# Graph attention on one core: a row of four edges in DRAM of 3088 bytes for 3136

## The chip, the cores and the metric

The kernel runs on one core of a Trainium2 chip. The metric is the device time of one execution in microseconds (us). A core has a matrix engine (TensorE, PE), a vector engine (VectorE, DVE), an engine for pointwise functions (ScalarE, ACT), a general one (GpSimd, POOL) and SyncE (SP), which here only issues transfers. 16 DMA engines move data between DRAM and the on-chip memory of 128 partitions.

## The reference

6250 nodes of 96 features, 200,000 edges (src, dst). Each edge takes a query from its source node and a key and a value from its target node; the softmax over the edges of a source node weighs the values.

```python
q = (embeds[rows] @ qW).reshape(e, HEADS, dh)      # rows = src, 4 heads of 24
k = (embeds[cols] @ kW).reshape(e, HEADS, dh)      # cols = dst
v = (embeds[cols] @ vW).reshape(e, HEADS, dh)
scores = jnp.clip(jnp.einsum('ehd,ehd->eh', q, k), -10.0, 10.0)
exp_s = jnp.exp(scores)
norms = jax.ops.segment_sum(exp_s, rows, num_segments=nvar)[rows]
w = exp_s / (norms + 1e-08)
res = jax.ops.segment_sum(w[:, :, None] * v, rows, num_segments=nvar).reshape(nvar, d)
...
x = _layernorm(x + embeds + res)                   # embeds is x
```

The edges come sorted by dst. The sums are over src, so the kernel sorts them again.

## The kernel before

**Part one (to about 170 us).** x is projected to q, k and v. k and v go to a table in DRAM (`kv3`), q stays on chip. At the same time the edges are counted by tile of 128 source nodes. SP also clears the last block of each of 49 tiles in `rows_dram` with 49 transfers of `pad_rows` (`clear`), a tensor of one row a partition.

**Part two (to about 840 us).** 112 groups of 1792 edges, two groups a turn, 56 turns. Every edge gets a place: edges of the same tile lie together, in runs of four (`RUN`). For each group a window of 128 table rows is loaded (`window_of`, L798, 144 KB; SP issues it once PE is done with the window before it), and the local numbers of the targets are broadcast to all partitions (L822, 1024 KB a turn). PE picks k and v by matmuls with a 0/1 matrix (L1188), ACT writes them from PSUM into `payload` (L937) and beside them the tag, the source node's number in its tile (L933). `payload` holds for two turns (p) and two groups (u) 16 columns of `WROW` floats on each partition: k, v (2 x 96 floats), the tag at `TAG` = 192, and what is left up to `WROW`. Four columns, one run, are one row in DRAM: `rows_dram` has `RUN * WROW` floats a row. POOL scatters them with an indirect DMA (L654), 128 rows each, four to a group, eight to a turn, 448 in all. A group's `payload` is written again two turns later, once its scatters have landed.

**Part three (from about 840 us).** The 472 blocks of 128 rows are read in 236 pairs (L842, 392 KB each, ring `blk` of 8 pairs, a place free when POOL's message of its last pair is made). For each pair ACT copies the tags (L972), DVE makes the 0/1 matrix of tags (L1611), PE turns it (L1261) and fetches q (L1271), DVE forms q times k (L1625) and sums it (L1634), ACT takes exp (L979), POOL multiplies v by it (L716), PE sums over the edges (L1250) and DVE adds the sums to `acc` (L1601). Each step runs some pairs behind the one before (`lagged`). At the end the layer norm and the stores.

All of `work`'s tiles, `payload` and `blk` among them, are cut one behind the other out of one tensor, so that those behind them begin where they end. Before its first scatter POOL waits for the table and the clears, sets the floats of `payload` behind the tag to zero (L635) and waits for that.

Of the kernel before, what the change touches and what calls it, by code (L numbers as in the profile page):

```python
# [25 lines left out]
P = 128  # L26
# [5 lines left out]
COLS = 14  # L32
QUAD = 2
RUN = 4
RB = 4
NCH = RB * RUN
HC = 2
KPART = 4
TSLOT = 4
WROW = 196  # L40
TAG = 192
BLK = 4
PAIR = 2
# [18 lines left out]
def gnn_program(nc, x, src, dst, wq, wk, wv, out):  # L62
# [3 lines left out]
    NT = -(-N // P)  # L66
# [12 lines left out]
    KPARTS = NCH // KPART  # L79
# [3 lines left out]
    NBLK = NPAIR * PAIR  # L83
    FULL = MOST_RUNS // P
    NBATCH = NG // HG
    PIECES = NBATCH // PB
# [12 lines left out]
    TI = FULL_NT // TSLOT  # L99
# [6 lines left out]
    assert COLS * P + (RUN - 1) * NB <= RUNS * RUN <= 2048 and SORTED < FAR and NBLK < 2048  # L106
    assert RUN == 1 << RUN_BITS and P == 1 << P_BITS and NCH == KPARTS * KPART and EDGE_ROWS < ITERS - 1
    assert NG == HG * NBATCH and NBATCH % PB == 0 and NB <= HI * LO and HROWS <= P and TT <= P and NT <= CLEARS * (TI + 1)
    assert RB == KPARTS and RUN == KPART and FULL + NT <= NBLK and FULL <= 512 and PIECES == 7 and TI == 12 and COLS * P <= 2048


    HEAD_SLOT = 1
# [8 lines left out]
    kv3 = nc.dram_tensor("kv3_table", (NTAB, 3 * 2 * D), BF16).ap()  # L121
    rows_dram = nc.dram_tensor("sorted_rows", (SORTED, RUN * WROW), F32).ap()
    local_dram = nc.dram_tensor("sorted_local", (2, QUAD * NCH, P), F16).ap()

    with ExitStack() as ctx:
        def sb(name, shape, dt):
            return ctx.enter_context(nc.sbuf_tensor(name, shape, dt))

        def sem(name):
            return ctx.enter_context(nc.semaphore(name))  # L130
# [21 lines left out]
        blk_row = sb("blk_row", [P, NBLK], F16)  # L152
        pad_rows = sb("pad_rows", [P, RUN * WROW], F32)

# [26 lines left out]
        def share(at, shape, dt):  # L181
            n = 1
            for d in shape:
                n *= d
            words = -(-n // 2) if dt in (BF16, F16) else n
            assert at + words <= WORK, (at, words)
            top[0] = max(top[0], at + words)
            v = work[:, at:at + words]
            v = v if dt == F32 else v.bitcast(dt)
            v = v[:, 0:n]  # L190
            if len(shape) == 1:
                return v, at + words
            names = " ".join(f"d{i}" for i in range(len(shape)))
            return v.rearrange(f"p ({names}) -> p {names}",
                               **{f"d{i}": d for i, d in enumerate(shape)}), at + words


        payload, at = share(0, [2, QUAD, NCH, WROW], F32)
        far_rows, at = share(at, [NCH // 2, 2, 3, D], BF16)
# [88 lines left out]

        blk, at = share(0, [SBI, PAIR, BLK, WROW], F32)
        tags, at = share(at, [SBI, CH, TWIN], BF16)  # L290
# [7 lines left out]

        sq_all, _ = share(SBI // 2 * PAIR * BLK * WROW, [NT, D], F32)
        assert NT * D <= SBI // 2 * PAIR * BLK * WROW and NPAIR <= SBI * (JS - 1) + SBI // 2  # L300
        inv = pad_rows[:, 0:NT * HEADS].rearrange("p (t h) -> p t h", t=NT)
# [56 lines left out]
        pads_made = sem("pads_made")  # L358
# [198 lines left out]
        def _(pool):  # L557
# [74 lines left out]
                pool.wait_ge(table_out[n], 16 * (TI // 2))  # L632
            pool.wait_ge(rest_out, 32)
            pool.wait_ge(tails_out, 16 * NT)
            pool.memset(payload[:, :, :, :, TAG + 1:WROW].rearrange("p o u c w -> p (o u c) w"), 0.0).then_inc(pads_made, 1)  # L635
            pool.wait_ge(pads_made, 2)
            last_place = pool.to_reg(SORTED - 1)
            last_row = pool.to_reg(NTAB - 1)

# [1092 lines left out]
```

## Time and profile before

| | |
|---|---|
| median of 3 runs | 1666.95 us (1665.98 to 1668.39) |
| profiled execution | 1672.0 us, its span 1670.2 us |
| PE busy | 1465.2 us, 88% |
| DVE busy | 1431.4 us, 86% |
| ACT busy | 1019.1 us, 61% |
| POOL busy | 912.8 us, 55% |
| moved by the DMA engines | 465.03 MB, mean 278 GB/s |

Busy shares are means over parts with different limits, so the parts have to be read one by one. The granted clock of PE was 0.95 of full speed in the mean.

### The profile page before, as it was taken

The numbers are of one execution on the slowest core, as the hardware profiler recorded it, in microseconds if no ns is written. First come the engines' busy times: TensorE is split into PE (matmuls) and PEld (weight loads), VectorE is DVE, ScalarE is ACT, GpSimd is POOL, SyncE is SP. The second block draws the span as 40 slices with busy tenths as digits, with TensorE's granted clock in tenths as the row PEclk, the third lists the DMA queues.
The fourth block names the chain that finished last, engine by engine and source line by source line (L and its number), as shares of the span: only waits on it lengthen the run. The fifth ranks groups of instructions, "written<-read, shape, count | busy, mean of one in ns | idle before, by whom it ended". The sixth has DMA issues, their size and how long they took to land.

```text
span 1670.2 us, 56304 instructions
## 1 busy us (share of the span) xinstructions
PE 1465.2 (88%) x19964; PEld 1407.4 (84%) x19965; DVE 1431.4 (86%) x2940; ACT 1019.1 (61%) x1836; POOL 912.8 (55%) x768
## 2 busy tenths in 40 slices
PE   5854988898888888888769999999999999999992
PEld 3744878787787878888769999999999999999992
DVE  5889999898988998899258888888888888888897
ACT  4342666566666665666546666666666666666665
POOL 6240777677767777777734444444444444444442
PEclk8566999999999999999979999999999999999996
DMA  7672999999999999899979767677777777777742
GB/s 222 221 274 102 352 367 354 346 331 374 355 328 357 358 357 338 348 364 355 351 286 299 240 241 246 237 248 240 243 247 238 244 245 239 246 242 240 247 157 58
DMA packets 159483, 465.03 MB, mean 278 GB/s; under 512 B 37026, under 2 KB 59298, under 8 KB 152276
## 3 DMA queue, kind: packets, MB, share of 16 engines
q1 hardware_dynamic: 120916, 300.70, 54.2%
q0 software_dynamic: 35840, 163.36, 24.1%
q10 hardware_dynamic: 2688, 0.46, 0.2%
q8 instruction: 23, 0.38, 0.1%
q14 instruction: 16, 0.13, 0.0%
HBM read 271.21 MB, written 209.73 MB: 288 GB/s over the span
## 4 chain that ended last, share of the span: by engine, by line
PE 76%; DVE 10%; issue 7%; DMA 4%; SPq 1%; ACT 1%; DVEq 0%; POOL 0%; POOLq 0%; ACTq 0%
PE two_a L1188 13%; PE meta L1250 13%; PE sum_bank L1250 12%; PE two_b L1188 11%; PE two_a L1271 7%; PE two_b L1271 7%; PE one_d L1261 3%; PE one_c L1261 3%; DMA work<-kv_table 2%; PE meta L1206 2%; PE one_d L1217 2%; DVE work L1523 1%; DVE work L1530 1%; PE sum_bank L1170 1%; DVE cols_work L1368 1%
## 5 line engine op out<-in xcount | busy, mean ns | idle before, releaser
L654 POOL DMA_INDIRECT sorted_rows<-work x448 | 498.9, 1114 | 210.4 <-issue 144.5
L716 POOL TENSOR_TENSOR work<-work 128x768 f32<-128x768 f32 x236 | 352.2, 1492 | 440.7 <-ACT work L979 440.7
L1188 PE MATMUL two_a<-work 128*128 128x192 bf16 x2688 | 265.1, 249 | 88.6 <-issue 86.1
L1188 PEld LDWEIGHTS two_a<-work 128*128 128x128 f16 x2688 | 217.0, 99 | 109.5 <-issue 89.5
L937 ACT ACTIVATE work<-two_a 128x768 f32<-128x768 f32 x224 | 181.5, 810 | 150.0 <-PE two_a L1188 148.2
L1188 PE MATMUL two_b<-work 128*128 128x192 bf16 x2688 | 264.7, 250 | 0.0
L988 ACT ACTIVATE work<-work 128x1024 f32<-128x1024 bf16 x236 | 247.2, 1048 | 0.0
L1250 PE MATMUL sum_bank<-work 128*128 128x100 f32 x1888 | 235.9, 278 | 3.6 <-DVE acc L1601 3.6
L1250 PE MATMUL meta<-work 128*128 128x100 f32 x1888 | 235.9, 278 | 0.9 <-DVE acc L1601 0.9
L1634 DVE TENSOR_REDUCE work<-work 128x32 f32<-128x768 f32 x236 | 225.0, 953 | 8.2
L1188 PEld LDWEIGHTS two_b<-work 128*128 128x128 f16 x2688 | 223.1, 99 | 6.3
L1250 PEld LDWEIGHTS sum_bank<-work 128*128 128x128 f32 x1888 | 219.8, 192 | 4.0 <-issue 3.9
L1250 PEld LDWEIGHTS meta<-work 128*128 128x128 f32 x1888 | 219.6, 192 | 1.3 <-issue 1.2
L979 ACT ACTIVATE work<-work 128x32 f32<-128x32 f32 x236 | 54.1, 229 | 261.6 <-DVE work L1618 261.6
L937 ACT ACTIVATE work<-two_b 128x768 f32<-128x768 f32 x224 | 181.7, 811 | 46.4 <-PE two_b L1188 45.3
L1611 DVE TENSOR_TENSOR work<-work,node_row 128x1024 bf16<-128x1024 bf16 x236 | 163.4, 692 | 20.6 <-ACT work L972 20.6
L1625 DVE TENSOR_TENSOR work<-two_a,work 128x768 f32<-128x768 f32 x118 | 113.0, 958 | 41.7 <-PE two_a L1271 41.6
L1625 DVE TENSOR_TENSOR work<-two_b,work 128x768 f32<-128x768 f32 x118 | 113.0, 958 | 40.8 <-PE two_b L1271 40.8
L1271 PE MATMUL two_a<-q,work 128*128 x2832 | 141.1, 207 | 2.3 <-ACT work L985 2.3
L1271 PE MATMUL two_b<-q,work 128*128 x2832 | 140.3, 207 | 0.0
L1271 PEld LDWEIGHTS two_a<-q,work 128*128 128x128 bf16 x2832 | 129.5, 98 | 3.1 <-issue 2.9
L1271 PEld LDWEIGHTS two_b<-q,work 128*128 128x128 bf16 x2832 | 129.2, 98 | 0.0
(235 smaller groups left out, 2186.6 us busy)
## 6 DMA issues: line engine op xcount, KB each, us to landing
work<-sorted_rows SPq DMA_DIRECT2D x472, 392.0 KB, 3.5
work<-sorted_local SPq DMA_DIRECT2D x56, 1024.0 KB
sorted_rows<-pad_rows SPq DMA_DIRECT2D x49, 392.0 KB, 4.6
work<-kv_table SPq DMA_DIRECT2D x112, 144.0 KB
sorted_rows<-work POOLq DMA_INDIRECT x448
kv_table<-work SPq DMA_DIRECT2D x12, 576.0 KB, 3.4
work<-in_x SPq DMA_DIRECT2D x12, 192.0 KB, 4.4
out<-acc SPq DMA_DIRECT2D x6, 384.0 KB
```

Source lines behind the costliest of these rows:

```text
L654: pool.indirect_dma_start(out=rows_dram, out_offset=bass.IndirectOffsetOnAxis(ap=place_now[:, p, u, b:b + 1], axis=0), in_=payload[:, p, u ...
L716: pool.tensor_tensor(now[:, :, 0:D].rearrange("p c (h f) -> p c h f", h=HEADS), blk[:, k, :, :, D:2 * D].rearrange("p m c (h f) -> p (m c) ...
L937: act.activation(payload[:, p, u, KPART * part:KPART * (part + 1), 0:2 * D].rearrange("p (b k) w -> p b k w", b=2), kv_ps[part % 2], ACT.C ...
L979: act.activation(msg[:, k % MSGS, :, D:AW], clipped[:, k], ACT.Exp).then_inc(exp_made[k % PSEM], 1)
L988: act.activation(hot_f[:, k % HOTF], hot[:, k % HOTS], ACT.Copy).then_inc(hotf_made[k % PSEM], 1)
L1188: mm = pe.matmul(to, picked[:, u % 2, k * P:(k + 1) * P], window[:, u, :, n, :], start=(n == 0), stop=(n == 2))
L1250: mm = pe.matmul(sums[k % 2][:, m, :], hot_f[:, k % HOTF, m * BLK + c, :], msg[:, k % MSGS, m * BLK + c, :], start=(c == 0), stop=(c == BL ...
L1261: mm = pe.transpose(turned[k % 2][:, c, :], hot[:, k % HOTS, c, :], ident_b[:])
L1271: mm = pe.matmul(q_ps[k % 2][:, m, c, :], hot_T[:, k % 2, m * BLK + c, :], q3[:, bass.ds(tile, 1), i, :].rearrange("p a d -> p (a d)"), st ...
L1611: dve.tensor_tensor(hot[:, k % HOTS].rearrange("p c (n i) -> p c n i", i=TWIN), tags[:, k].unsqueeze(2).to_broadcast([P, CH, P // TWIN, TW ...
L1625: dve.tensor_tensor(qk.rearrange("p (m c) d -> p m c d", m=PAIR), q_ps[k % 2], blk[:, k, :, :, 0:D], ALU.mult).then_inc(qk_made[k % PSEM], 1)
L1634: dve.tensor_reduce(score[:, k], qk.rearrange("p c (h f) -> p (c h) f", h=HEADS), AX.X, ALU.add).then_inc(score_made[k % PSEM], 1)
```

## The change

An edge's row is 193 floats, k, v and tag, for 196. Four of them are 772 floats (3088 bytes) for 784 (3136 bytes). With that `payload`, `blk`, `pad_rows` and `rows_dram` shrink, and everything cut out behind them moves. The memset of the floats behind the tag, and POOL's wait for it, are gone. An assertion keeps `WROW` at `TAG + 1`.

```diff
@@ -37,7 +37,7 @@
-WROW = 196
+WROW = 193
 TAG = 192
...
-            pool.memset(payload[:, :, :, :, TAG + 1:WROW].rearrange("p o u c w -> p (o u c) w"), 0.0).then_inc(pads_made, 1)
-            pool.wait_ge(pads_made, 2)
             last_place = pool.to_reg(SORTED - 1)
             last_row = pool.to_reg(NTAB - 1)
```

No instruction changes its place. POOL's program ahead of its first scatter, before; 784 is the length of a row in floats:

```order
L630 TENSOR_LOAD flag_i [waits tables_made]
L630 ISA x2
L635 MEMSET work 128x64x3 [waits rest_out,tails_out,table_out1,table_out0]
L700 COMPARE_AND_BRANCH [waits pads_made]
L701 UNCONDITIONAL_BRANCH
L701 ISA
L654 DMA sorted_rows<-work 60416x784 [waits place_made0,tag_kept0,pay0_made0]
L654 DMA sorted_rows<-work 60416x784 [waits pay1_made0]
```

And in the changed kernel, where lines from 635 on stand two lines higher:

```order
L630 TENSOR_LOAD flag_i [waits tables_made]
L630 ISA x2
L698 COMPARE_AND_BRANCH [waits rest_out,tails_out,table_out1,table_out0]
L699 UNCONDITIONAL_BRANCH
L699 ISA
L652 DMA sorted_rows<-work 60416x772 [waits place_made0,tag_kept0,pay0_made0]
L652 DMA sorted_rows<-work 60416x772 [waits pay1_made0]
```

The memset and the wait for `pads_made` are gone, the waits for the table and the clears stand at the branch, and the scatters carry rows of 772 floats.

## Rows read from the trace of the kernel before

**Rows 1.** The page: tenths of DMA share in 40 slices of the span, and GB/s.

```profile
DMA  7672999999999999899979767677777777777742
GB/s 222 221 274 102 352 367 354 346 331 374 355 328 357 358 357 338 348 364 355 351 286 299 240 241 246 237 248 240 243 247 238 244 245 239 246 242 240 247 157 58
```

**Rows 2.** Stretches of the span: busy us and instructions of each engine, granted clock, DMA.

```profile
core 0: us, PE busy (x) PEld busy (x) DVE busy (x) ACT busy (x) POOL busy (x), PEclk, DMA share, GB/s
0.00:130.00 130.00, 84.59 (x308) 65.01 (x309) 100.84 (x148) 56.74 (x71) 55.41 (x77) 0.68 0.70 240
...
960.00:1600.00 640.00, 640.00 (x9279) 640.00 (x9278) 567.32 (x1160) 425.70 (x774) 288.10 (x194) 1.00 0.71 243
...
200.00:800.00 600.00, 519.26 (x7338) 488.49 (x7337) 539.32 (x1183) 370.79 (x640) 443.04 (x396) 0.98 0.96 352
955.00:1600.00 645.00, 645.00 (x9361) 645.00 (x9360) 571.61 (x1171) 428.49 (x781) 289.74 (x195) 1.00 0.71 243
```

**Rows 3.** The chain that ended last, 955 to 1600 us, shares by line.

```profile
by line: PE sum_bank L1250 27.8%; PE meta L1250 27.8%; PE two_b L1271 15.5%; PE two_a L1271 15.3%; PE one_c L1261 6.8%; PE one_d L1261 6.7%
```

**Rows 4.** Waits from 200 to 800 us: us in total, times, longest.

```profile
ACT work L937 <- PE two_a L1188: 131.7, 183, 4.0
POOL sorted_rows L654 <- issue: 97.0, 294, 2.1
...
PE two_a L1188 <- issue: 75.4, 45, 3.0
ACT work L937 <- PE two_b L1188: 39.5, 191, 1.1
POOL sorted_rows L654 <- DVE work L1502: 35.1, 32, 3.0
...
POOL sorted_rows L654 <- ACT work L937: 25.2, 70, 1.5
```

**Rows 5.** Timeline of one turn: start us, us, instruction, idle before.

```profile
601.00 0.33 SPq L822 DMA_DIRECT2D work<-sorted_local  x1
...
606.73 6.49 SPq L798 DMA_DIRECT2D work<-kv_table  x2
...
614.36 1.15 PE L1188 MATMUL two_a<-work 128*128 128x192 bf16 x12 [1.56 <-issue]
```

**Rows 6.** The page's queue of the scatters: packets, MB, share of 16 engines.

```profile
q0 software_dynamic: 35840, 163.36, 24.1%
```

**Rows 7.** The queue of SP's loads from 955 to 1600 us.

```profile
q1 hardware_dynamic: 56118, 156.47, 71.1%
```

**Rows 8.** The queue of the 8 KB stores from 200 to 800 us.

```profile
q10 hardware_dynamic: 2352, 0.40, 0.4%
```

**Rows 9.** Timeline of POOL around its first scatter.

```profile
130.66 0.26 POOL L635 MEMSET work<- 128x192 f32 x1 [2.53 <-DMA kv_table<-work]
164.64 1.33 POOL L654 DMA_INDIRECT sorted_rows<-work  x1 [33.72 <-issue]
```

**Rows 10.** What SP's queue waited for, 0 to 200 us.

```profile
SPq L777 <- POOL work L620: 64.6, 11, 13.5
```

**Rows 11.** Pieces of the chain at the start of part three: start us, us.

```profile
844.72 6.17 DMA work<-sorted_rows
...
892.94 4.39 DMA work<-sorted_rows
```

**Rows 12.** Groups that read or write edge rows: busy us, mean ns, idle before.

```profile
L716 POOL TENSOR_TENSOR work<-work 128x768 f32<-128x768 f32 x236 | 352.2, 1492 | 440.7 <-ACT work L979 440.7
...
L937 ACT ACTIVATE work<-two_a 128x768 f32<-128x768 f32 x224 | 181.5, 810 | 150.0 <-PE two_a L1188 148.2
...
L1625 DVE TENSOR_TENSOR work<-two_a,work 128x768 f32<-128x768 f32 x118 | 113.0, 958 | 41.7 <-PE two_a L1271 41.6
...
L972 ACT ACTIVATE work<-work 128x16 bf16<-128x16 f32 x236 | 48.8, 207 | 16.1 <-DMA work<-sorted_rows 16.1
...
L933 ACT ACTIVATE work<-work 128x16 f32 (+1 forms) x112 | 25.4, 227 | 35.5 <-DMA work<-sorted_local 31.0 <-ACT work L952 4.5
```

**Rows 13.** Waits from 955 to 1600 us.

```profile
POOL work L716 <- ACT work L979: 355.4, 195, 1.9
```

More of the change, by code:

```diff
@@ L108, in gnn_program @@
     assert NG == HG * NBATCH and NBATCH % PB == 0 and NB <= HI * LO and HROWS <= P and TT <= P and NT <= CLEARS * (TI + 1)
-    assert RB == KPARTS and RUN == KPART and FULL + NT <= NBLK and FULL <= 512 and PIECES == 7 and TI == 12 and COLS * P <= 2048
+    assert WROW == TAG + 1 and RB == KPARTS and RUN == KPART and FULL + NT <= NBLK and FULL <= 512 and PIECES == 7 and TI == 12 and COLS * P <= 2048
     HEAD_SLOT = 1
```

## The prediction

> **What bounds the kernel now.** I read the line of DMA shares over the span first, then the stretches, the chain of waits and the queue tables of two stretches. The run has three parts. Up to 170 us the edges are counted and ordered. From 170 to 840 us the edge rows are built and scattered to DRAM (56 turns, 12 us each). From 840 us on the rows are read back and summed [rows 1, 2].
>
> In the third part PE is busy in all of its 640 us, every step of the chain is a PE group, and the DMA engines work at 0.71 [rows 2, 3]. Whatever a load of rows gains or loses there does not reach the end, as long as the DMA share stays below 1: 147 ns a row (below) could become 207.
>
> In the second part PE is busy 519 of 600 us, DVE 539, POOL 443, and the DMA engines 0.96 of the time at 352 GB/s [rows 2]. The reader should see where PE's missing 81 us stand: 75.4 us lie in 45 waits ahead of L1188, nearly one for each of the 49.5 turns, put down to "issue" [rows 4]. One such wait shows what it is. SP issues the window of the second group at 606.73 us, right after PE ended that group's previous work; PE starts the group at 614.36 us, 1.56 us after it ran dry [rows 5]. A window is 144 KB, and in the same ring stands the broadcast of 1,024 KB issued at 601.00, while POOL puts eight scatters, 163.36 MB / 56 = 2.9 MB, in each turn into the other ring [rows 6]. So PE waits for its window because the 16 DMA engines are full. POOL isn't the limit: its 443.0 us of scatter instructions and 97.0 us of gaps of 0.3 us between them are 540 of 600 us, and it waited 60.3 us for DVE and ACT [rows 2, 4]. Hence a turn is about as long as its DMA work.
>
> **The scatter, the term of the sum.** The scatters' queue (q0) moved 163.36 MB, which is 52,092 rows of 3,136 bytes, and took 24.1% of the engines' span: 0.241 x 1670.2 = 402.5 us [rows 6]. That is 402.5 x 16 / 52,092 = 123.6 ns of one engine a row. A row of 3,088 bytes is 48 bytes, 1.53%, shorter. No row of this trace shows a transfer of rows whose length isn't a multiple of 64 bytes (x rows are 384 bytes, table rows 1,152, broadcast rows 8,192), so I bound it.
>
> - If time goes by bytes in all of it: 402.5 x 0.0153 = 6.2 us less.
> - If a part is a fixed price of a packet: of the 35,840 packets of q0, 448 x 16 are completions, and 28,672 are left, four to an engine and scatter, of 52,092 / 28,672 = 1.82 rows and 402.5 x 16 / 28,672 = 224.6 ns each (two rows, less those out of bounds). The loads of the third part are one row a packet: 0.711 x 645 us x 16 / 49,895 rows (156.47 MB) = 147.1 ns [rows 7]. From row + packet = 147.1 and 1.82 rows + packet = 224.6 come 95 ns for a row and 52 for a packet. This is an estimate, the two stretches having different neighbours. 1.53% of 95 ns is 1.45 ns, and 52,092 x 1.45 / 16 = 4.7 us less.
> - If the engine moves pieces of which the 48 bytes don't save one: 0. Rows of 3,088 bytes start at any multiple of 16 bytes, and touch 49 pieces of 64 bytes wherever they start, as many as 3,136 bytes do.
> - On the other side: each row now begins or ends inside a piece of 32 bytes that it shares with its neighbour. What a write of a part of a piece costs no row shows. The nearest is the smallest packet: queue q10 (256-byte rows and completions) took 0.4% of 600 us on 16 engines for 2,352 packets, 16.3 ns each [rows 8]. One more such piece a row is 52,092 x 16.3 / 16 = 53 us more.
>
> I take 4.7 us, since it is built on the rows nearest to it, both packets of the same row length. Of it the part counts in which the engines are the limit, by their share 0.96: **4.5 us less**, 0.08 us of each turn. PE's wait of 1.6 us a turn is large enough to give it back. When the wait is shorter, PE's own 10.5 us a turn comes next, far off.
>
> **The removed memset, and its wait.** It took 0.26 us, and the first scatter began 33.7 us after it, when the first rows were ready [rows 9]. POOL has nothing else to do in between: 0. It also covers the lost wait for `pads_made`, of which nothing else hangs behind. If this cover were gone it would be 0.26 us and a wait, once.
>
> **The clears.** 49 blocks of pad rows shrink by 0.3 MB in all, in the first part, where the DMA engines work at 0.70 [rows 2] and SP waits for POOL's table parts (64.6 us at L777) rather than for a queue [rows 10]: 0.
>
> **The start of the third part.** Here loads stand on the chain: 6.17 us for the first block and 4.39 us at 893 us, where SP's load of x shares the engines [rows 11]. 1.5% of 10.6 us is 0.2 us less.
>
> **The compute engines.** Rows of an edge now start every 772 bytes for 784, so most no longer start on 16 bytes. Nobody's count of elements changes. L937 writes such rows (810 ns), L716 and L1625 read them (1492 and 958 ns), L933 and L972 touch their tags (227 and 207 ns) [rows 12]. No row shows them off 16 bytes; ends are nothing and, say, their slack. In part two ACT waits 171 us for PE before L937, about 0.43 us for each of its 396, so it may take half as long again. In part three POOL waits 355.4 / 195 = 1.8 us a pair [rows 13], and DVE is idle 73 us of 645, 0.38 us a pair [rows 2]. With PE at 100% none of this is seen: 0. Tiles laid out behind the rows move by 768 bytes, tensors behind `pad_rows` by less; none changes its shape: 0. An odd 0.4 us more in L1625 would be the first thing to show.
>
> **Sum.** 4.5 + 0.2 = 4.7 us less. The profiled execution took 1672.0 us, of which 1670.2 are its span; it would take 1667.3. Taken off the median of the runs, 1666.95 (the profiled one is 0.3% above it), the forecast is 1662.2 us.
>
> **Rivals.**
> A. *The forecast* (time by bytes): 1660.5 to 1663.6. For it speaks the DMA share of 0.96 with PE waiting in nearly every turn; against it, that two thirds of a gain of 0.3% are already enough to vanish below what can be told from no change.
>
> B. *Nothing to measure*, in two ways. The row's time goes by pieces, worth 0 to 3 us. For example, if the engine also handles the bytes between a row's start and the 256-byte boundary below it, the mean start is 96 bytes above it before (rows start at 0, 64, 128, 192) and 120 after (at any multiple of 16), so 3,232 bytes become 3,208; 0.74% of 95 ns is 0.70 ns a row, 2.3 us in all, and the time 1664.6. Or PE's wait is the latency of the window in its ring and not the engines' load; then 1667. Against the latter speaks that a window of 144 KB took 7.6 us [rows 5].
>
> The first of these is a rule of the Trainium skill: "DMA: Bandwidth & Descriptors", section "How a descriptor splits into AXI transactions", has reads fetched from the 256-byte boundary below their start, with unused bytes that still cost. No row of this trace shows whether that is so; the chance of B holds it.
>
> C. *Slower*: the writes of part two now end inside shared pieces, and the memory or the engine must read the piece before it writes. The place is the scatter, 52,092 rows; the third part reads only. It decides from 1.45 + 1.0 = 2.5 ns a row, beyond which the kernel is over 3.3 us slower. At a third of the small packet's price, 5.4 ns, it is 52,092 x 3.95 / 16 = 13 us more, 1680; at the whole price 48 us more, 1715. For it speaks that no write of before met such a piece and that the engines have no idle time in which to hide one [rows 2]; against it, that it is one piece in about 97, and may be read where the engine doesn't wait for it.
>
> The Trainium skill speaks for C in "Collectives: The Full Stack", section "Rules for kernel authors": it asks for buffers aligned to 32 bytes because that prevents a read-modify-write in the hardware. It names no price, and every row written before starts at a multiple of 64, so the trace can't say.
>
> That the change doesn't do what it says can be left out: the scatters and loads have 772 elements a row for 784.
>
> **How the numbers follow.** About 0.2%, 3.3 us, is what a measurement of this kernel can tell from no change. A has 0.42 and is faster. B has 0.30 and lies within. C has 0.28 and is slower, 0.12 of it beyond 1685, since the small packet's price is an upper end. The low end is by bytes in all, 1666.95 - 6.2 - 0.2 = 1660.5, less the 1 us by which runs of one kernel differ: 1659. The high end of 1685 takes in C up to 18 us more (7 ns a row gross), which leaves out 0.12 above and about 0.05 below. The likeliest is A.
>
> **What would show it.** Right: q0's bytes 160.9 MB and its share near 23.8%; the 600 us of part two at the same share 0.96 with 0.08 us less a turn; the first load of rows from DRAM some 5 us earlier than 844.7; all of part three unchanged at 3.31 us a pair, and its DMA share 0.70. Wrong: q0's time a row above 124 ns, with PE's waits before L1188 longer than 75 us in 600 (C); q0's time a row at 123 to 124 ns (B, pieces); q0's share down and the turn unchanged (B, latency); a DMA share well above 0.71 in part three, or PE no longer at 100% there (a cost on the reads that I gave no chance).

## The result: slower, by 0.2 to 0.6%

| | before | changed |
|---|---|---|
| median of 5 runs each | 1668.39 us | 1677.86 us |
| ratio | | 1.0057 (95%: 1.0038 to 1.0075) |
| profiled execution, span | 1672.0, 1670.2 us | 1677.9, 1676.1 us |
| beside each other again, on another chip | 1671.46 us | 1673.85 us |
| ratio | | 1.0021 (1.0007 to 1.0035) |

The forecast was 1662.2 us and faster. Both comparisons have the changed kernel slower; they differ in how much.

The profile of the changed kernel, queue of the scatters on the page (packets, MB, share of 16 engines over the span), the same packets as in [rows 6], 2.5 MB less, and yet more time:

```profile
q0 software_dynamic: 35840, 160.86, 24.4%
```

0.244 x 1676.1 = 409.0 us x 16 / 52,092 rows are 125.6 ns a row, for 123.6 before.

Stretches of the span (columns as in [rows 2]), and the queue of SP's loads from 955 to 1600 us:

```profile
200.00:800.00 600.00, 520.26 (x7301) 489.91 (x7301) 533.80 (x1172) 368.06 (x635) 438.67 (x392) 0.97 0.95 345
955.00:1600.00 645.00, 645.00 (x9362) 645.00 (x9359) 571.38 (x1171) 428.47 (x780) 289.91 (x195) 1.00 0.72 239
```

```profile
q1 hardware_dynamic: 56158, 154.17, 72.4%
```

In these 600 us of part two POOL issued 392 scatters for 396, and the engines moved 345 GB/s for 352 at a share of 0.95 for 0.96. That is this one execution: in another of the same kernel (e6 below) it was 397 scatters and 350 GB/s at 0.96. Part three takes its 3.31 us a pair as before, PE without a gap. But its loads are dearer too: 154.17 MB are 49,926 rows, 0.724 x 645 x 16 / 49,926 = 149.7 ns a row for 147.1 [rows 7]. PE does not wait for that in this stretch.

The groups of the engines have not moved: L714, L935 and L1623 (L716, L937 and L1625 before) take what they took in [rows 12].

```profile
L714 POOL TENSOR_TENSOR work<-work 128x768 f32<-128x768 f32 x236 | 352.7, 1495 | 441.9 <-ACT work L977 441.9
...
L935 ACT ACTIVATE work<-two_a 128x768 f32<-128x768 f32 x224 | 181.6, 811 | 154.4 <-PE two_a L1186 151.2
...
L1623 DVE TENSOR_TENSOR work<-two_a,work 128x768 f32<-128x768 f32 x118 | 112.9, 957 | 41.8 <-PE two_a L1269 41.8
```

Where this execution lost time shows in the scatters' own line (duration ns min/median/max, first and last start in us), first of the kernel before, then of the changed one:

```profile
L654 POOL DMA_INDIRECT sorted_rows<-work x448: 967/975/1907, 164.6 to 839.3; - x150
```

```profile
L652 POOL DMA_INDIRECT sorted_rows<-work x448: 967/975/1905, 164.3 to 843.4; - x150
```

Of 5.9 us by which the span is longer, 4.4 arise between the first and the last scatter, 679.1 us for 674.7. The rest is behind the last scatter. The chain of waits of the changed kernel there (start us, us):

```profile
848.90 6.09 DMA work<-sorted_rows
...
887.24 9.69 SPq L847
...
899.48 4.03 DMA work<-sorted_rows
```

Before, the same issue of x's last rows (L849) stood 7.24 us on the chain, so 2.4 us were lost there in this execution:

```profile
883.15 7.24 SPq L849
```

Two more profiles, e6 (the changed kernel again) and e1 (nearly the same, both below), do not repeat this picture. From the first to the last scatter they took 672.0 and 671.3 us, less than before, and behind the last scatter 835.1 and 835.8 us for 830.9 (the first profile of the changed kernel: 832.7). In both, 3 to 4 us of that is PE busy for longer on the same work, with a granted clock of 0.97 from 900 to 960 us where before it was 1.00. So no place for the loss is shown.

```profile
L652 POOL DMA_INDIRECT sorted_rows<-work x448: 966/976/2706, 164.9 to 836.9; - x150
```

```profile
L652 POOL DMA_INDIRECT sorted_rows<-work x448: 967/976/1930, 164.4 to 835.7; - x150
```

So the question is why 48 bytes less a row, 1.5% of the largest stream of part two, where DMA looked like the limit, save nothing.

### The profile page after: what moved, and what is told of

The parts are those of the page before. It is cut to its first block, busy times and chain, and to the rows that moved or that the text cites. A ratio compares the mean times of both kernels' runs of the same rounds, so it can differ in the third digit from the quotient of the medians.

```text
span 1676.1 us, 56303 instructions
## 1 busy us (share of the span) xinstructions
PE 1465.8 (87%) x19964; PEld 1408.8 (84%) x19965; DVE 1430.6 (85%) x2940; ACT 1018.8 (61%) x1836; POOL 913.3 (54%) x767
## 3 DMA queue, kind: packets, MB, share of 16 engines
q0 software_dynamic: 35840, 160.86, 24.4%
## 4 chain that ended last, share of the span: by engine, by line
PE 79%; DVE 8%; issue 7%; DMA 4%; SPq 1%; ACT 1%; POOL 0%; DVEq 0%; POOLq 0%; ACTq 0%
PE two_a L1186 14%; PE two_b L1186 13%; PE meta L1248 12%; PE sum_bank L1248 12%; PE two_a L1269 7%; PE two_b L1269 7%; PE one_c L1259 3%; PE one_d L1259 3%; DMA work<-kv_table 3%; PE meta L1204 2%; PE one_d L1215 2%; PE sum_bank L1168 1%; DVE cols_work L1366 1%; PE sum_bank L1087 1%; DMA work<-sorted_rows 1%
## 5 line engine op out<-in xcount | busy, mean ns | idle before, releaser
L714 POOL TENSOR_TENSOR work<-work 128x768 f32<-128x768 f32 x236 | 352.7, 1495 | 441.9 <-ACT work L977 441.9
L1186 PEld LDWEIGHTS two_a<-work 128*128 128x128 f16 x2688 | 218.3, 99 | 112.0 <-issue 91.9
L935 ACT ACTIVATE work<-two_a 128x768 f32<-128x768 f32 x224 | 181.6, 811 | 154.4 <-PE two_a L1186 151.2
L935 ACT ACTIVATE work<-two_b 128x768 f32<-128x768 f32 x224 | 181.7, 811 | 47.7 <-PE two_b L1186 46.6
L1623 DVE TENSOR_TENSOR work<-two_a,work 128x768 f32<-128x768 f32 x118 | 112.9, 957 | 41.8 <-PE two_a L1269 41.8
L1623 DVE TENSOR_TENSOR work<-two_b,work 128x768 f32<-128x768 f32 x118 | 113.0, 958 | 40.9 <-PE two_b L1269 40.9
```

The lines of the kernel that those rows point to most:

```text
L714: pool.tensor_tensor(now[:, :, 0:D].rearrange("p c (h f) -> p c h f", h=HEADS), blk[:, k, :, :, D:2 * D].rearrange("p m c (h f) -> p (m c) ...
L935: act.activation(payload[:, p, u, KPART * part:KPART * (part + 1), 0:2 * D].rearrange("p (b k) w -> p b k w", b=2), kv_ps[part % 2], ACT.C ...
L1186: mm = pe.matmul(to, picked[:, u % 2, k * P:(k + 1) * P], window[:, u, :, n, :], start=(n == 0), stop=(n == 2))
L1623: dve.tensor_tensor(qk.rearrange("p (m c) d -> p m c d", m=PAIR), q_ps[k % 2], blk[:, k, :, :, 0:D], ALU.mult).then_inc(qk_made[k % PSEM], 1)
```

## Experiments

Each was run beside the kernel before on one chip; the kernels of one comparison share their runs of before. All of the layouts below except e6, e1, e10 and e14 come out of one rewriting of the changed kernel, in which the four pitches are numbers of their own (below with the changed kernel's values). In e2, e3, e4, e7 and e16 an edge has 193 floats in a run, and what a run or a row has beyond 772 is padding at its end, zeroed once. In e5, e11, e12, e13 and e15 it has 192 and no tag, so that their sums over edges are meaningless, while the instructions keep their sizes. And in e2, e3, e4, e7, e12 and e16 POOL multiplies a pair (L714) in two instructions of half the size, which takes 317 us of the 645 of part three for 290. No run has this split together with the layout of before, so a small difference of these kernels to before can be the split's.

```diff
+PAY_PITCH = 772    # a run of four edges on chip, part two
+BLK_PITCH = 772    # the same, part three
+ROW_PITCH = 772    # a row in DRAM, and what a scatter moves
+LOAD = 772         # what a load of part three moves of it
...
-    rows_dram = nc.dram_tensor("sorted_rows", (SORTED, RUN * WROW), F32).ap()
+    rows_dram = nc.dram_tensor("sorted_rows", (SORTED, ROW_PITCH), F32).ap()
-        payload, at = share(0, [2, QUAD, NCH, WROW], F32)
+        payload, at = share(0, [2, QUAD, RB, PAY_PITCH], F32)
...
-        blk, at = share(0, [SBI, PAIR, BLK, WROW], F32)
+        blk, at = share(0, [SBI, PAIR, BLK_PITCH], F32)
...
-                        in_=payload[:, p, u, b * RUN:(b + 1) * RUN, :].rearrange("p k w -> p (k w)"), in_offset=None,
+                        in_=payload[:, p, u, b, 0:ROW_PITCH], in_offset=None,
```

The expectations weigh theories by letter. D, S: a start off 32 bytes costs, in DRAM or on chip. L: a length that is no multiple of 32 costs. B: the shift of the other tensors costs. G: such a start costs on either side, and a row over 3072 bytes costs one piece more. P: the stretches of 256 bytes touched in DRAM set a row's time. Y: its bytes do. M: only a row of whole such stretches is cheap.

All results together. "Stretches" is the number of 256-byte stretches of DRAM, counted from multiples of 256, that a row touches in the mean over all rows; it is worked out from the pitch, and takes it that the tensor starts on such a multiple, which no trace shows. "Part two" is the time from the start of the first scatter to that of the last, in one profile each. ns are engine time a row from the shares of the two queues in the same profile. The changed kernel and e1 give 124.8 to 125.6 and 149.7 to 150.1, and e5, e10 and e14, whose DMA rows are alike, 120.4 to 122.0 and 146.4 to 147.5: a difference under 1.5 ns says little.

| kernel | bytes a row | stretches | part two, us | scatter, load ns | time to before (95%) |
|---|---|---|---|---|---|
| before | 3136 | 13 | 674.7 | 123.6, 147.1 | 1 |
| changed, again (e6) | 3088 | 13 | 672.0 | 125.3, 149.9 | 1.0021 (1.0007 to 1.0035) |
| e1 | 3088 | 13 | 671.3 | 124.8, 150.1 | 1.0018 (1.0005 to 1.0031) |
| e2 | 3136 | 13 | 675.9 | 123.7, 149.6 | 1.0004 (0.9993 to 1.0015) |
| e3 | 3088 | 13 | 669.8 | 124.1, 148.4 | 1.0014 (1.0002 to 1.0026) |
| e4 | 3104 | 13 | 669.9 | 123.0, 148.3 | 1.0002 (0.9987 to 1.0017) |
| e7 | 3136, loads 3088 | 13 | 673.7 | 123.5, 149.2 | 0.9999 (0.9982 to 1.0016) |
| e16 | 3200 | 13 | 672.9 | 125.7, 152.8 | 1.0044 (1.0026 to 1.0062) |
| e11 | 3008 | 12.5 | 663.9 | 118.8, 146.3 | 0.9955 (0.9941 to 0.9970) |
| e5 | 3072 | 12 | 654.9 | 120.4, 146.4 | 0.9883 (0.9864 to 0.9902) |
| e12 | 3072 | 12 | 652.6 | 120.2, 147.3 | 0.9899 (0.9881 to 0.9917) |
| e15 | 2944 | 12 | 656.3 | 116.3, 142.7 | 0.9883 (0.9861 to 0.9906) |
| e13 | 2816 | 11 | 638.7 | 112.0, 138.1 | 0.9799 (0.9785 to 0.9813) |
| e10 | 3072 | 12 | 654.5 | 122.0, 147.5 | 0.9914 (0.9894 to 0.9933) |
| e14 | 3072 | 12 | 654.0 | 121.4, 147.3 | 0.9894 (0.9876 to 0.9912) |

The scatters' lines of e12, e11, e13 and e16 (those of e5 and e15 stand with their runs):

```profile
L663 POOL DMA_INDIRECT sorted_rows<-work x448: 967/978/1904, 165.3 to 817.9; - x150
```

```profile
L663 POOL DMA_INDIRECT sorted_rows<-work x448: 966/975/1907, 163.9 to 827.8; - x150
```

```profile
L663 POOL DMA_INDIRECT sorted_rows<-work x448: 968/982/1894, 165.1 to 803.8; - x150
```

```profile
L664 POOL DMA_INDIRECT sorted_rows<-work x448: 969/977/1907, 165.5 to 838.4; - x150
```

By stretches, part two took 669.8 to 679.1 us at 13 (nine profiles, the changed kernel's first among them), 663.9 at 12.5, 652.6 to 656.3 at 12 (five profiles) and 638.7 at 11.

### Which side, which length

**e2**, only the starts on chip off 32 bytes:

```diff
+PAY_PITCH = 788
+BLK_PITCH = 788
+ROW_PITCH = 784
+LOAD = 784
```

> Rows in DRAM are 784 floats (3136 bytes, starts at multiples of 64 bytes) and 784 floats are moved, as before; on chip a run of four edges (193 floats each, 12 of padding behind them) starts every 788 floats (3152 bytes), at any multiple of 16 bytes. POOL's message of a pair is two instructions of half the size. Theory D (the start in DRAM costs): a row takes 123.6 ns on the scatters' queue and 147 ns on the loads' in part three, as before, and the time is that of before within 0.2%. Theory S (the start on chip costs): 125.6 and 149.7 ns, 6 to 10 us slower than before. Theory L (the length costs, 3088 bytes being no multiple of 32): as before.

Measured: 1.0004, the scatter at 123.7 ns as before, the load at 149.6 for 147.1. So the load is 2.5 ns dearer, through the starts on chip or POOL's split instruction, and the scatter, which reads there, shows nothing. Theory S falls as the cause of the lost time: the kernel is as fast as before. The queue of loads of e2 from 955 to 1600 us, with the same row length as in [rows 7]:

```profile
q1 hardware_dynamic: 56100, 156.43, 72.3%
```

**e3**, only the starts in DRAM off:

```diff
+PAY_PITCH = 784
+BLK_PITCH = 784
+ROW_PITCH = 772
+LOAD = 772
```

> Rows in DRAM are 772 floats (3088 bytes), as in the changed kernel; on chip a run starts every 784 floats, at a multiple of 32 bytes. Theory D: as the changed kernel, 125.6 ns a row for the scatter, 149.7 for a load, 6 to 10 us slower than before. Theory S: faster than before by 4.5 us, at 122.2 ns a row and 145.7. Theory L: as the changed kernel.

Measured: 1.0014, 124.1 and 148.4 ns. It is not the gain of 4.5 us that S asked for. It is a loss of 2.3 us, less than the 6 to 10 of D. With starts on chip in order, 48 bytes less still save nothing.

**e4**, a row of 3104 bytes, every start in DRAM and of runs on chip on 32 bytes (all pitches 776):

> A row is 776 floats, 3104 bytes or 97 x 32, in DRAM and on chip (193 floats an edge, 4 of padding to a run), so that every start is a multiple of 32 bytes and half of them of 64. Theories D, S and L with a piece of 32 bytes: nothing is shared, and the 32 bytes saved show: 122.6 ns a scattered row, 146 a loaded one, 3 us faster than before. With a piece of 64 bytes: 124.5 to 125.6 and about 149, 4 to 9 us slower.

Measured: 1.0002, 123.0 and 148.3 ns. 32 bytes less and nothing shared in any piece of 32: no loss, and no gain either. Whether the 0.2% that the changed kernel is slower lie between 3104 and 3088 isn't shown, since the intervals overlap.

**e6**, the changed kernel again, and **e1**, the changed kernel with the tensors behind `pad_rows` where they were:

```diff
-        pad_rows = sb("pad_rows", [P, RUN * WROW], F32)
+        pad_rows = sb("pad_rows", [P, RUN * 196], F32)
...
-                    sp.dma_start(of_block(FULL + b), pad_rows[:]).then_inc(tails_out, 16)
+                    sp.dma_start(of_block(FULL + b), pad_rows[:, 0:RUN * WROW]).then_inc(tails_out, 16)
```

> The changed kernel again, beside the others on the chip of this comparison. Theory G (a start off 32 bytes costs on either side, and a row over 3072 bytes costs one piece more): 125.6 ns a scattered row, 149.7 a loaded one, 6 to 10 us slower than before, while the two kernels with only one side off 32 bytes were 0 and 2 us slower. If it is as fast as before here, the first result was the chip's scatter.

> The changed kernel, but with pad_rows as wide as before (784 floats), so that all tensors behind it start where they did, at multiples of 64 bytes rather than 32 bytes past one. Rows are 3088 bytes in DRAM and on chip. Theory B (the shift of the other tensors costs): 123 ns a scattered row and the time of before or 3 us less. Theory G: nothing changes against the changed kernel, 125.6 and 149.7 ns, 6 to 10 us slower than before.

Measured: 1.0021 and 1.0018. B falls: where the other tensors lie doesn't matter. The changed kernel is slower here too, by less than the 6 to 10 us expected (2.4). The scatters of e6 take the share that they took in the first profile of the changed kernel:

```profile
q0 software_dynamic: 35840, 160.86, 24.4%
```

**e7**, everything at multiples of 64 bytes, only the loads 3088 bytes long (all pitches 784):

```diff
+LOAD = 772
```

> Rows in DRAM and on chip start every 784 floats, at multiples of 64 bytes, and the scatter moves 784 floats; the loads of part three move the first 772 floats of each (3088 bytes), which are all that is used. Theory L (the length of 3088 costs by itself): 149.7 ns a loaded row. Theory G: 146.5 ns, under the 147.1 of before, as nothing is off a boundary. The time within 0.2% of before, since part three is bound by PE.

Measured: 0.9999, as expected, and 149.2 ns a loaded row, where G had 146.5. G is wrong on this: a load that is 48 bytes shorter is 2.1 ns dearer, with every start in order. That speaks for the length by itself (L), but POOL's split instruction is in e7 too. It is in e12 and not in e5, at 3072 bytes, and there the two differ by 0.9 ns. Loads of e7 from 955 to 1600 us:

```profile
q1 hardware_dynamic: 56162, 154.18, 72.2%
```

### What a shorter row can give

**e5** leaves the tag out of the row, so that a row is 3072 bytes (all pitches 768; ACT writes tags to a tensor that nobody reads):

```diff
-WROW = 193
-TAG = 192
+WROW = 192
+TAG = 191
...
+        tag_side = sb("tag_side", [P, NCH], F32)
```

> A row is 768 floats, 3072 bytes or 48 x 64, k and v alone: tags are written to a side tile and part three takes the last element of v in their place, so the sums over edges are left meaningless while all instructions keep their sizes. All starts are multiples of 64 bytes. It prices bytes by themselves: if my split into 95 ns a row and 52 ns a packet holds, 64 bytes are 1.9 ns, so 121.7 ns a scattered row, and the time is 6 us below before. If the DMA's time isn't what sets a turn, the row gets cheaper and the time stays.

Measured: 0.9883, which is 19.6 us off 1673.2 (18.0 by the medians), three times what I expected, at 120.4 ns a row. From 3088 to 3072 bytes are 16 bytes, and 1.4% of the time. Bytes don't explain that. Two things change at 3072: all rows lie on multiples of 1024, and a row of 12 x 256 bytes touches 12 stretches of 256 and not 13. A line of the stretches of the span, and the scatters' line, of e5:

```profile
200.00:800.00 600.00, 527.20 (x7523) 496.92 (x7520) 542.89 (x1192) 380.50 (x659) 458.54 (x409) 0.99 0.97 358
```

```profile
L663 POOL DMA_INDIRECT sorted_rows<-work x448: 971/975/1907, 164.4 to 819.3; - x150
```

409 scatters in 600 us for 396, and the last one starts 20 us earlier: all of the gain is in part two.

**e12** has rows of 3072 bytes in DRAM but starts on chip at any multiple of 16 (pitches 772 on chip, 768 in DRAM):

> As the kernel with rows of k and v alone (3072 bytes, tags left out, so that the sums over edges are meaningless), except that on chip a run starts every 3088 bytes, at any multiple of 16. In DRAM all rows start at multiples of 1024 bytes. POOL's message is two instructions of half the size. If the gain of 1.2% came from length or from DRAM: 1.2% faster than before again, 120.4 ns a scattered row, 149 a loaded one. If it came from the starts on chip: as before.

Measured: 0.9899, the same gain within the intervals. It comes from the length or from DRAM, not from the starts on chip.

**e11** moves 3008 bytes of each run, **e13** 2816 (pitches 768 on chip):

```diff
+ROW_PITCH = 752    # e13: 704
+LOAD = 752         # e13: 704
```

> Rows of 752 floats, 3008 bytes or 47 x 64, moved from and to runs that start every 3072 bytes on chip; tags and the last 16 floats of v of every fourth edge are left out. Rows start at multiples of 64 in DRAM, so that 2 in 4 of them reach over one 256-byte boundary more than at 3072. Theory P (pieces between 256-byte boundaries set a row's time: 13 at 3136, 12 at 3072, 12.5 here): slower than 3072 by about 5 to 10 us, 121 ns a scattered row. Theory Y (bytes set it, and 64 of them are 3 ns and 19 us): 117.5 ns, 2.3% faster than before, unless POOL's issue holds it at about 1.7%.

> Rows of 704 floats, 2816 bytes or 11 x 256, from runs that start every 3072 bytes on chip; tags and the last 64 floats of every fourth edge are left out. Theory P: 11 pieces for 12 at 3072. Theory Y: 10% fewer bytes than before. Both: about 110 ns a scattered row. The time tells what comes next when the DMA's work shrinks: POOL issues 448 scatters at 1.12 + 0.30 us, 636 us for part two against 655 at 3072, so the time ends near 1635 and not at 1600, and DMA's share falls under 0.93.

Measured for e11: 0.9955. **64 bytes fewer than 3072, and slower than it**, by 0.6% of the time (e12, in the same comparison). Theory Y (bytes) falls; 12.5 stretches lie between 12 and 13 in time too, and in part two: 663.9 us between 652.6 (e12) and 674.7 (before). But the engine time of a row doesn't follow: 118.8 ns at 3008, less than the 120.4 at 3072. The shares of packet time aren't what sets a turn. One of the stretches of e11:

```profile
200.00:800.00 600.00, 524.97 (x7441) 495.00 (x7439) 540.30 (x1186) 375.50 (x651) 451.13 (x404) 0.98 0.96 349
```

Measured for e13: 0.9799, 1637.5 us for the expected 1635. Its waits of POOL from 200 to 800 us say what comes next:

```profile
POOL sorted_rows L663 <- issue: 99.4, 326, 0.3
POOL sorted_rows L663 <- ACT work L948: 15.2, 50, 0.3
POOL sorted_rows L663 <- DVE work L1513: 13.1, 43, 0.3
```

No gap is longer than 0.3 us, which is the gap between any two scatters. POOL was busy 471.68 us in it, and with the gaps that is the whole of 600 us: the issue of 448 scatters is the bound, some 33 us under before. The share of DMA stayed at 0.96, where I had expected under 0.93. So a share of 0.96 doesn't by itself say that the engines are the limit: here POOL is.

```profile
200.00:800.00 600.00, 540.10 (x7683) 508.16 (x7681) 545.35 (x1200) 393.16 (x674) 471.68 (x421) 0.99 0.96 346
```

**e15** moves 2944 bytes, which touch 12 stretches as 3072 do (ROW_PITCH and LOAD 736); **e16** has rows of 3200 bytes, which touch 13 as 3136 do (all pitches 800, the clears' zeros read in two halves):

> Rows of 736 floats, 2944 bytes or 46 x 64, from runs that start every 3072 bytes on chip; tags and the last 32 floats of every fourth edge are left out. In DRAM rows start at 0 or 128 past a multiple of 256 and touch 12 stretches of 256 bytes each, as many as at 3072, while 3008 touches 12.5 in the mean. Theory P (stretches of 256 bytes touched in DRAM set the time): 1.1% faster than before, as 3072, and faster than 3008, which was 0.45%. Theory Y (bytes, with a peculiarity at 3008 or 3072): between 3008 and 2816 (2.0% faster), so 1.3% to 1.6%. Theory M (only a row that is a multiple of 256 long and starts on one is cheap, all others pay for an end within a stretch): near 3008, 0.5% to 0.8% faster.

> Rows of 800 floats, 3200 bytes or 50 x 64, in DRAM and on chip, 28 floats of padding to a run of four edges of 193. Rows start at 0 or 128 past a multiple of 256 and touch 13 stretches of 256 bytes, as many as 3136 does. The clears read their zeros in two halves of 400 floats. Theory P: within 0.2% of before, in spite of 64 bytes more. Theory Y: 1% slower, at 126 to 127 ns a scattered row. Theory M: 0.3% to 0.6% slower.

Measured for e15: 0.9883, to the digit what 3072 gave, with 128 bytes fewer, and 0.7% faster than 3008 with its 64 more. M falls for it (0.5 to 0.8% expected), Y misses (1.3 to 1.6%; the interval ends at 1.4%) and had fallen with e11, and P holds. POOL is near its bound there as well (409 scatters in 600 us, where it could issue 421), but not at it. For e16: 1.0044, where P had no change and Y had 1.0%, and 125.7 ns a row, near Y's 126. The 0.44% are 7 us, and its profile has them behind part two, which took 672.9 us for 674.7. From the last scatter on it took 839.4 us for 830.9, more than any other kernel here (the next has 836.1). The issue of x's last rows takes 12.10 us in it for 7.24, and PE was idle 10.0 us between the first and the last sum of part three, for 4.9 before (stretches, first of before, then of e16):

```profile
862.90:1641.70 778.80, 773.86 (x11180) 772.98 (x11178) 691.01 (x1404) 513.61 (x941) 355.18 (x240) 1.00 0.70 237
```

```profile
863.80:1649.20 785.40, 775.41 (x11180) 774.50 (x11177) 691.56 (x1404) 513.47 (x941) 389.22 (x474) 1.00 0.72 240
```

```profile
884.13 12.10 SPq L863
```

So P holds for the scatters of e16 in this profile, and what lengthens the start of part three stays open: dearer loads, POOL's split, other places of the tiles and finer clears are all in it. The scatters' line of e15, and the scatters' queue of e16:

```profile
L663 POOL DMA_INDIRECT sorted_rows<-work x448: 969/977/2574, 165.4 to 821.7; - x150
```

```profile
q0 software_dynamic: 35840, 166.69, 24.4%
```

### A version that keeps the tag and the short row

**e10**, from the changed kernel: the tag is one byte, written over the lowest byte of v's last element after a group's four parts.

```diff
-WROW = 193
-TAG = 192
+WROW = 192
+TAG = WROW - 1
...
-                    act.activation(payload[:, p, u, :, TAG], sorted_v[:, at_c, u, 0:NCH].rearrange("p o w -> p (o w)"),
-                                   ACT.Copy).then_inc(tag_kept[u % GSEM], 1)
                     for part in range(KPARTS):
                         group_done(act, kv_made[part], u, done_c)
                         ...
+                    for part in range(KPARTS):
+                        group_done(act, pay_made[part], u, done_c)
+                    act.activation(pay_bytes[:, p, u, :, 4 * TAG], sorted_v[:, at_c, u, 0:NCH].rearrange("p o w -> p (o w)"),
+                                   ACT.Copy).then_inc(tag_kept[u % GSEM], 1)
...
-                                       blk[:, k, :, :, TAG].unsqueeze(3).to_broadcast([P, PAIR, BLK, TWIN]), ACT.Copy
+                                       blk_bytes[:, k, :, :, 4 * TAG].unsqueeze(3).to_broadcast([P, PAIR, BLK, TWIN]), ACT.Copy
```

> A row is k and v alone, 3072 bytes, at multiples of 1024 bytes: ACT writes the tag as one byte over the lowest byte of v's last element (an error of 2 to the power -16 in it) after the four parts of a group, and part three reads the tag from this byte. The scatters of a group wait for its last part. If the short row was what gave 19 us with the tag left out: 1.0% to 1.2% faster than before, 120.4 ns a scattered row. If ACT's later tag stalls POOL, by up to 0.3 us for each of 112 groups, 33 us more, and the kernel is slower than before.

Measured: 0.9914, 1656.8 us for 1671.46. The short row's gain survives. It is 5 us less than e5 gave, but the intervals overlap, and its part two is as short (654.5 us for 654.9), so that POOL's wait for the late tag costs something isn't shown.

**e14** writes the tags in two halves:

```diff
+                    def tags_of(half):
+                        for part in (2 * half, 2 * half + 1):
+                            group_done(act, pay_made[part], u, done_c)
+                        at = slice(2 * KPART * half, 2 * KPART * (half + 1))
+                        act.activation(pay_bytes[:, p, u, at, 4 * TAG],
+                                       sorted_v[:, at_c, u, at].rearrange("p o w -> p (o w)"),
+                                       ACT.Copy).then_inc(tag_kept[half][u % GSEM], 1)
```

> The kernel with the tag in a byte of v (3072 bytes, 0.86% faster than before), with the tags written in two halves, after the third and the fourth part of a group, so that a scatter waits for half a group and not for all of it. One ACT instruction of 0.2 us more for each of 112 groups, and two semaphores counted together with others. If POOL's wait for the late tag cost the 5 us that it is behind the kernel without tags: 1.0% to 1.2% faster than before. If ACT's time costs it: 0.6% to 0.86%.

Measured: 0.9894, 1655.4 us for 1670.7, what e5 and e12 gave without a tag (0.9883 and 0.9899). The intervals of e10 and e14 overlap, so that the halves are better isn't shown. It is 1.1% faster than before. One of its stretches, and one tag write in a timeline of ACT:

```profile
200.00:800.00 600.00, 541.49 (x7538) 505.23 (x7538) 543.72 (x1195) 400.46 (x761) 453.23 (x409) 0.99 0.98 360
```

```profile
606.17 0.24 ACT L941 ACTIVATE work<-work 128x8 uint8 x1 [0.18 <-ACT work L948]
```

The path for edges whose targets span more than a window (`slow`) needs the tag written again by POOL. It has this write, but the inputs never take that path.

## Why the prediction was wrong

**The bound was right.** Part two follows its scatters' rows: from 3136 to 3072 bytes it became 20 us shorter, and part three kept its 3.31 us a pair. POOL wasn't the limit, and became it at 2816 bytes. The share of 0.96 that I took as proof is a weak one, since it stood there too. That the memset and its wait were worth nothing is in line with the first scatter, at 164.3 us without them for 164.6, and with e7 and e2, which have such a memset and take the time of before.

**The step that failed is the term of the sum: 48 of 3136 bytes, 1.53% of 95 ns a row.** I let the per-row time go by bytes and took its price by splitting two packet times. What the runs show is steps. At 13 stretches 3136, 3104 and 3088 bytes are the same or slower, with part two between 669.8 and 679.1 us in no order of length, and at 12 stretches 3072 and 2944 are the same. The prediction had the right ruler in its hand, in rival B, and laid it on wrong: it counted the bytes from the boundary below a row's start (3,232 to 3,208) and not how many boundaries a row reaches over. By count the answer was plain before any run: rows of 3136 start at 0, 64, 128 or 192 past a boundary and end at most at 3328 = 13 x 256; rows of 3088 start at up to 240 past one and end at 3328 as well. 13 before, 13 after, nothing saved. The Trainium skill, "DMA: Bandwidth & Descriptors", section "How a descriptor splits into AXI transactions", gives such a split as the vendor's account: whole transactions of 256 bytes and one for what is left, and where a read starts off a boundary, a first one from the boundary below, whose unused bytes still cost. In time the scatters follow the count of transactions, at 3008, 3072 and 2944 and in part two of 3200, although DRAM is the side that they write. The cost of unused bytes they don't show (next paragraph). On the chip's side, which the scatter reads, starts off every boundary changed nothing that shows (e12 against e5: part two 652.6 and 654.9 us). The loads, which do read DRAM, don't follow the count in ns a row: 146.3 at 3008, 146.4 at 3072 and 142.7 at 2944.

Other rulers do worse. By bytes alone rows of 2944 and of 3008 would both beat 3072. B's ruler, the bytes from the boundary below a row's start, gives much of the gain at 3072 (3,072 for 3,232 before, 15 us at the prediction's 95 ns a row) and puts 3008 behind it, but the sizes are off: from 3072 to 3008 bytes a row it has 32 bytes more, and part two took 9 us more (663.9 for 654.9); from 2944 to 3072 it has 64 more, and part two took no more; from 3088 to 3200 it has 56 more, again with nothing to see in part two. Stretches of 128 bytes would be 24 at 3008 as at 3072, and stretches of 512 would set 2944 (6.5) apart from 3072 (6). What isn't shown is the mechanism. In every run a scatter's pitch in DRAM is its length, so start and length never moved apart, and nothing here counts what the engine or the memory really handles.

**Rival C had the direction, and its mechanism isn't shown.** The scatter's row went from 123.6 to 125.6 ns, and against the 1.45 ns less that I had counted this is 3.4 ns, over the 2.5 from which C decides and under the 5.4 that I had priced. In time it was 9.5 us in the first comparison and 2.4 in the second, for C's 13. But C puts the loss into the scatters of part two, and of the three profiles of such a kernel only the first has it there (679.1, 672.0 and 671.3 us for 674.7). 3104 against 3088 bytes (1.0002 against 1.0021 and 1.0018) speaks for starts off 32 bytes, but the intervals overlap. e2 and e3 put more of it on DRAM's side than on the chip's (0.04 and 0.14%), again within their intervals. C said that the part that only reads is spared. It is not: a loaded row costs 2.6 ns more, and e7 has 2.1 of it with every start in order. It stayed hidden where PE was busy without a gap, as the first step said it would up to 207 ns; whether it is part of the longer start of part three is open.

**What I named as signs.** q0's bytes were 160.9 MB as said, its share 24.4% for 23.8; the first load of rows came at 848.9 us, 4 later and not 5 earlier (in e6 at 843.0); PE waited 76.8 us in 600, hardly more than 75.4. The sign for C, ns a row over 124, was met.

**The compute engines** were right: none was slower on the rows off 16 bytes (1495, 811 and 957 ns for 1492, 810 and 958).

The size of the loss stays open between 0.2 and 0.6%: both comparisons are of the same programs, and I found no row that tells them apart. Why it is a loss at all, and not nothing, stays open too.

## What to carry to other kernels

Before counting saved bytes of a row that is scattered to DRAM, count the 256-byte boundaries that its rows reach over, at all starts that the pitch gives: a shortening that leaves this count alone saved nothing here, and the last 16 bytes down to a multiple of 256 gave 1.4%. Where a row is a few bytes over such a size, look for a place for these bytes inside the row (here a tag in the lowest byte of a float, in e14 two instructions a group, 0.24 us each, of an engine with time to spare) rather than for padding or its removal. And check which engine is next: here the issue of scatters by POOL stopped the gain at 2%, with the DMA share still at 0.96.

## What the runs showed of the hardware

- A scatter of rows to DRAM went by the 256-byte stretches that its rows touch: part two took 669.8 to 679.1 us at 13 (3088, 3104, 3136 and 3200 bytes), 663.9 at 12.5 (3008), 652.6 to 656.3 at 12 (2944 and 3072).
- A load of 128 rows of 3088 bytes was dearer than one of 3136: 149.7 for 147.1 ns a row, and 149.2 with all starts on 64 bytes (e7, which also splits an instruction of POOL). At 3104 it was 148.3, at 3072 146.4 to 147.5.
- With starts on chip off 32 bytes a load of 3136 bytes took 149.6 for 147.1 ns a row (e2, which splits the same instruction), while reading there for a scatter cost nothing that shows (123.7 for 123.6).
- The packet time of a queue was no measure of what a turn costs: 3008 bytes had the shorter row (118.8 for 120.4 ns) and the longer time (0.9955 for 0.9883). And the engines' share was 0.96 where POOL's issue was the limit (e13).
- POOL issued an indirect scatter of 128 rows every 1.42 us at best in this kernel (421 in 600 us, e13).
- ACT wrote single bytes, one in 768 (a stride of an edge), at 0.24 us for 8 a partition (e14).
